# Two gated attentions and two feed-forward nets on one core: row maxima moved by DMA into the query tile, other lists for the first attention's engines, the second attention's first queries made in the FFN before it

## The reference

```python
q = x @ Wq.T + bq
k = context @ Wk.T + bk
v = context @ Wv.T + bv
...
scores = jnp.einsum('bhtd,bhcd->bhtc', q, k) / jnp.sqrt(jnp.asarray(d, x.dtype))
attn = jax.nn.softmax(scores, axis=-1)
out = jnp.einsum('bhtc,bhcd->bhtd', attn, v)
out = out.transpose(0, 2, 1, 3).reshape(B, T, D)
return out @ Wo.T + bo
```

## Time and profile before

| | us |
|---|---|
| median of 3 runs | 1145.16 |
| lowest and highest | 1142.67, 1146.78 |
| profiled execution | 1144.3 |
| its span in the trace | 1142.5 |
| granted PE clock, mean | 0.926 |

### The profile page before, as it was taken

How to read it: one execution, slowest core, us unless ns; L and a number is a source line. 1 busy time by engine, 2 the same in 40 slices (tenths; PEclk the granted TensorE clock), 3 DMA queues, 4 the chain that set the end, 5 groups by cost and what they waited for, 6 DMA issues and landing times. The chain is left out here.

```text
span 1142.5 us, 20567 instructions
## 1 busy us (share of the span) xinstructions
PE 987.9 (86%) x6833; PEld 864.7 (76%) x6833; DVE 792.5 (69%) x1588; ACT 626.8 (55%) x1088; POOL 235.1 (21%) x423
## 2 busy tenths in 40 slices
PE   6589999998659997826699995999999989999998
PEld 5367777776458876625588984899999977888888
DVE  5357888775339988979959833677777768656672
ACT  4156666665357779969748543556566544222230
POOL 4213333320139200000003303121111104111210
PEclk9699999999769999967689996999999998999999
DMA  6745554445042237779712376655656510000001
GB/s 200 220 107 140 134 133 116 128 121 163 1 159 111 111 123 223 252 254 325 258 45 100 126 240 137 165 119 118 127 127 132 123 38 1 20 19 33 23 19 38
DMA packets 102807, 143.60 MB, mean 126 GB/s; under 512 B 42950, under 2 KB 76742, under 8 KB 100438
## 3 DMA queue, kind: packets, MB, share of 16 engines
q1 hardware_dynamic: 102438, 141.67, 43.2%
q0 software_dynamic: 304, 1.10, 0.3%
HBM read 76.30 MB, written 47.13 MB: 108 GB/s over the span
## 5 line engine op out<-in xcount | busy, mean ns | idle before, releaser
L41 PE MATMUL bank<-f_xt_hi,f_w_hi 128*128 128x512 f32 x320 | 129.1, 404 | 14.3 <-DMA f_xt_lo<-x_spill 11.1
L43 PE MATMUL bank<-f_xt_hi,f_w_lo 128*128 128x512 f32 x320 | 126.5, 395 | 0.0
L42 PE MATMUL bank<-f_xt_lo,f_w_hi 128*128 128x512 f32 x320 | 126.3, 395 | 0.0
L2534 ACT ACTIVATE f_h<-bank,f_b 128x512 f32<-128x512 f32 x64 | 43.3, 690 | 121.8 <-PE bank L43 74.1
L595 ACT ACTIVATE a_prob<-bank 77x512 f32<-77x512 f32 x128 | 72.5, 591 | 31.5 <-PE bank L759 31.0
L661 DVE TENSOR_REDUCE a_maxima<-bank 128x4 f32<-128x308 f32 x128 | 60.4, 472 | 40.8 <-PE bank L734 40.5
L41 PEld LDWEIGHTS bank<-f_xt_hi,f_w_hi 128*128 128x128 f32 x320 | 61.2, 191 | 30.3 <-DMA f_xt_lo<-x_spill 13.5
L41 PE MATMUL bank<-f_w_hi,f_h_hi 128*128 128x256 f32 x256 | 72.6, 284 | 8.1 <-DVE xres L2499 8.1
L756 PE MATMUL bank<-a_stack,a_kb 96*77 96x256 f32 x256 | 70.8, 299 | 4.7 <-ACT a_mt L588 4.7
L43 PE MATMUL bank<-f_w_hi,f_h_lo 128*128 128x256 f32 x256 | 72.3, 282 | 0.0
L42 PE MATMUL bank<-f_w_lo,f_h_hi 128*128 128x256 f32 x256 | 72.3, 282 | 0.0
(11 more groups left out here) (299 smaller groups left out, 3081.1 us busy)
## 6 DMA issues: line engine op xcount, KB each, us to landing
u_spill<-f_ubuf SPq DMA_DIRECT2D x48, 256.0 KB, 2.6
f_uback<-u_spill SPq DMA_DIRECT2D x24, 512.0 KB, 5.8
a_stack<-a_queries SPq DMA_DIRECT2D x16, 512.0 KB, 4.8
a_q_max<-a_q_hi SPq DMA_DIRECT2D x32, 256.0 KB, 5.0
a_kb<-a_key_spill SPq DMA_DIRECT2D x96, 77.0 KB, 2.5
f_mats<-in_low_steps SPq DMA_DIRECT2D x12, 512.0 KB, 6.8
xres<-in_x SPq DMA_DIRECT2D x16, 256.0 KB, 4.4
a_queries<-a_q_hi SPq DMA_DIRECT2D x16, 256.0 KB, 2.6
```

Source lines behind the costliest of these rows:

```text
L41: nc.tensor.matmul(out, w_hi, m_hi, start=start, stop=False)
L42: nc.tensor.matmul(out, w_hi, m_lo, start=False, stop=False)
L43: return nc.tensor.matmul(out, w_lo, m_hi, start=False, stop=stop)
L2534: act.activation(h[:, n % 2, :], hbank[n % 4][:, :], ACT.Gelu, bias=b1[:, n:n + 1]).then_inc(h_ready, 1)
```

## The change

1. `stack` and `kb` have their free rows 96 to 111 filled: `kb` with the picks (once, in the set-up, by ACT for both halves of the double buffer), `stack` with the maxima. ACT copies the maxima as before and then issues a DMA that writes them to all 8 pairs of heads, 128 KB. A head's scores are one matmul over 112 rows; `s0` waits for that DMA instead of the copy. `pick` and its memset, and the memset of `mt`, go.
2. `PE_SLOT`, `ACT_SLOT`, `DVE_SLOT` and `POOL_SLOT` have another order, and the slots before batch 0 have lists of their own with the order that they had.
3. `fw` sends one of twelve pieces of the quantised weights, 196 KB, in each of the slots 1 to 12.
4. The layer norm, transpose and query products of the second attention's batch 0 are made in the quantised net's last block; the steps in `late_attention` return at once for batch 0. The half of `kz` that batch 0 uses is cleared and filled there as well, and the keys in `kz` and in `kb` have separate semaphores. The memset of `q_max` stands at the start of the block.

```diff
-                act.activation(pick[0:HEADS, :, :], pick_raw[:], ACT.Copy).then_inc(picked, 1)
+                for par in range(2):
+                    act.activation(kb[ROWS:FULL, par, :, :, :],
+                                   pick_raw[ROWS:FULL, :, :].rearrange("p (q a) s -> p a q s", a=2),
+                                   ACT.Copy).then_inc(picked, 1)
...
-        PE_SLOT = "s0 s1 t3 xt p1 s2 mx0 at0 s3 t0 mx1 s4 p3 mx2 s5 mx3 t1 pr0 s6 mx4 pr1 p5 mx5 s7 mx6 q0 p7 mx7 q1 mt t2".split()
-        ACT_SLOT = "s0 s1 p1 s2 at0 s3 p3 xt s4 s5 s6 st2 p5 s7 xn p7 mt q1".split()
-        DVE_SLOT = "w0 norm w1 mx0 w2 as mx1 mx2 xs mx3 ln mx4 w3 pu mx5 st1 mx6 am mx7 w4 w5 qs".split()
-        POOL_SLOT = "ln st1 xn".split()
+        PE_SLOT = "mx0 xt t3 mx1 s0 s1 mx2 s2 s3 p1 s4 mx3 s5 p3 mx4 s6 s7 at0 mx5 q0 mx6 q1 p5 mx7 pr0 t0 mt pr1 t1 t2 p7".split()
+        ACT_SLOT = "xt s0 s1 s2 s3 p1 s4 s5 st2 s6 at0 p3 q1 mt p5 s7 xn p7".split()
+        DVE_SLOT = "mx0 w0 w1 mx1 norm mx2 ln mx3 xs w2 mx4 w3 mx5 w4 as mx6 w5 mx7 qs am pu st1".split()
+        POOL_SLOT = "ln xn st1".split()
...
+                for what in early if isinstance(b, int) and b < 0 else order:
                     if what[0] == "w":
                         if not isinstance(b, int) or 0 <= b < FW_PIECES:
                             step(what, b, par)
                     elif what == "fw":
-                        if isinstance(b, int) and b == FW_PIECES:
-                            step(what, b, par)
+                        if not isinstance(b, int) or 1 <= b <= FW_PIECES:
+                            step(what, b - 1, 1 - par)
...
-                    sp.wait_ge(fw_done, FW_PIECES)
-                    for n in range(3):
-                        sp.dma_start(ffn["quantised"][:, n, :], fw[:, n * FW:(n + 1) * FW]).then_inc(fw_sent, 16)
-
-            slots(sp, SP_SLOT, step)
-            sp.wait_ge(fw_sent, 48)
+                    sp.wait_ge(fw_done, b + 1)
+                    sp.sem_inc(sp_passed, 1)
+                    n = fw_code.shape[1]
+                    sp.dma_start(ffn["quantised"].rearrange("p n f -> p (n f)")[:, bass.ds(b * n, n)],
+                                 fw[:, bass.ds(b * n, n)]).then_inc(fw_sent, 16)
+
+            slots(sp, SP_SLOT, step, SP_SLOT)
+            sp.wait_ge(fw_sent, 16 * FW_PIECES)
...
                     act.activation(mt[0:HEADS, par, :], MX[0:HEADS, 0:T], ACT.Copy).then_inc(mt_copied, 1)
+                    act.wait_ge(mt_copied, b + 1)
+                    act.dma_start(stack[ROWS:FULL, par, :, :].bitcast(F32),
+                                  mt[0:HEADS, par, :].bitcast(F32).unsqueeze(1).to_broadcast([HEADS, PAIRS, T]),
+                                  ).then_inc(mt_moved[par], 16)
...
                     if n == 0:
-                        pe.wait_ge(mt_copied, b + 1)
+                        wait_turn(pe, mt_moved, 16, b, par)
                         if isinstance(b, int) and b == 0:
-                            pe.wait_ge(picked, 1)
-                            pe.wait_ge(cleared, 3)
+                            pe.wait_ge(picked, 2)
                     if not (isinstance(b, int) and b == 0 and n < 2):
 
                         pe.wait_ge(probs, b * PAIRS + n - 1)
                     for half in range(2):
                         pair, a = pair_of(2 * n + half)
                         out = (S0, S1)[n % 2][0:S, half * T:(half + 1) * T]
-                        pe.matmul(out, kb[0:ROWS, par, a, pair, 0:S], stack[0:ROWS, par, pair, :],
-                                  start=True, stop=False)
-
-                        last = pe.matmul(out, pick[:, 2 * pair + a, 0:S], mt[:, par, :], start=False, stop=True)
+                        last = pe.matmul(out, kb[0:FULL, par, a, pair, 0:S], stack[0:FULL, par, pair, :],
+                                         start=True, stop=True)
                     last.then_inc(scores, 1)
...
-                    for a in range(HPC):
-                        sp.dma_start(kz[own[a], par, :, a, :].bitcast(F32),
-                                     late["k_dram"][own[a], 0, :, bass.ds(b * S, S)]).then_inc(keys_in[par], 16)
+                    for a in range(HPC if not (isinstance(b, int) and b == 0) else 0):
+                        sp.dma_start(kz[par][own[a], :, a, :].bitcast(F32),
+                                     late["k_dram"][own[a], 0, :, bass.ds(b * S, S)]).then_inc(kz_in[par], 16)
+                    if isinstance(b, int) and b < 2:
+                        sp.wait_ge(picked, b + 1)
...
+                    if i == 1:
+                        pool.wait_ge(ocoded, late["values_free"] - 4)
+                        pool.memset(late["kz0"][:].bitcast(F32), 0.0).then_inc(first.kz_cleared, 1)
+                pool.wait_ge(first.cleared, 3)
+                pool.wait_ge(first.ln_stats, 1)
+                pool.tensor_tensor(first.nmean[:], first.zero[:], first.mv[:, :, 0], ALU.subtract)
+                pool.tensor_tensor(first.var[:], first.mv[:, :, 1], first.eps[:], ALU.add).then_inc(first.ln_eps, 1)
+                pool.wait_ge(first.ln_eps, 1)
+                pool.tensor_tensor(first.rstd[:], first.var[:], first.minus_half[:], ALU.pow).then_inc(first.ln_rstd, 1)
+                pool.wait_ge(first.ln_rstd, 1)
+                pool.tensor_tensor(first.nmr[:], first.nmean[:], first.rstd[:], ALU.mult).then_inc(first.ln_nmr, 1)
...
+                    if i == 2:
+                        sp.wait_ge(first.kz_cleared, 1)
+                        for n in range(2):
+                            sp.wait_ge(k_saved[n], 16 * NK)
+                        for a in range(2):
+                            half = slice(a * P // 2, (a + 1) * P // 2)
+                            sp.dma_start(late["kz0"][half, :, a, :].bitcast(F32),
+                                         late["k_dram"][half, 0, :, 0:S]).then_inc(first.kz_in[0], 16)
...
+                    if b == 12:
+                        dve.wait_ge(e_added, 1)
+                        for t in range(TT):
+                            last = dve.bn_stats(first.bn[:, t, :], xres[:, t, :])
+                        last.then_inc(first.ln_bn, 1)
+                        dve.wait_ge(first.ln_bn, 1)
+                        for t in range(TT):
+                            last = dve.bn_aggr(first.mv[:, t, :], first.bn[:, t, :])
+                        last.then_inc(first.ln_stats, 1)
+                    if b == 14:
+                        dve.wait_ge(first.xt_rounded, 1)
+                        dve.tensor_tensor(xt_lo, T1[:, :].rearrange("p (c t) -> p c t", c=DC), xt_hi.bitcast(F32),
+                                          ALU.subtract).then_inc(first.xt_split, 1)
...
+                    if b == 14:
+                        act.wait_ge(first.ln_nmr, 1)
+                        for t in range(TT):
+                            last = act.activation(xn[:, t, :], xres[:, t, :], ACT.Identity,
+                                                  bias=first.nmr[:, t:t + 1], scale=first.rstd[:, t:t + 1])
+                        last.then_inc(first.ln_xn, 1)
+                    if b == 16:
+                        act.wait_ge(first.xt_ready, 1)
+                        act.activation(xt_hi, T1[:, :].rearrange("p (c t) -> p c t", c=DC), ACT.Copy).then_inc(first.xt_rounded, 1)
...
+                    if b == 14:
+                        pe.wait_ge(first.ln_xn, 1)
+                        pe.wait_ge(v_done, 7)
+                        for c in range(DC):
+                            for t in range(TT):
+                                last = pe.transpose(T1[:, c * T + t * P:c * T + (t + 1) * P],
+                                                    xn[:, t, c * P:(c + 1) * P], ident[:])
+                        last.then_inc(first.xt_ready, 1)
+                pe.wait_ge(first.xt_split, 1)
+                pe.wait_ge(l_split["wq"], 1)
+                pe.wait_ge(v_done, 8)
+                pe.wait_ge(e_added, B - 1)
+                for n in range(2):
+                    for c in range(2):
+                        cols = slice((2 * n + c) * P, (2 * n + c + 1) * P)
+                        for kc in range(DC):
+                            last = three_passes(nc, (T0, X0)[n][:, c * T:(c + 1) * T], late["wq_hi"][:, kc, cols],
+                                                late["wq_lo"][:, kc, cols], xt_hi[:, kc, :],
+                                                xt_lo[:, kc, :], kc == 0, kc == DC - 1)
+                    last.then_inc(first.q_ready, 1)
```

122 lines of the change are left out of this document (76 added, 46 removed).

## The result

The changed kernel is slower. It takes 1164.8 us in the median of four runs (1158.81 to 1172.57), beside 1145.97 for the kernel before in the same comparison; the ratio is 1.0156, with a 95% interval of 1.0121 to 1.0191. The forecast was 1125, the range ended at 1138, and the time lies 27 us above it. The profiled execution took 1162.29 us with a span of 1160.5, 18.0 more than the span of 1142.5 before, at a mean granted clock of 0.899 instead of 0.926.

A forecast was written before the change was run, and what follows sets the result against it. PE was taken to set the pace, busy 14.34 of a 15.0 us slot, DVE next. Terms -22.5 + 1.1 + 0.5 - 1.0 - 0.5 (keys' wait) + 2.1 = -20.3 gave 1125 us, range 1114 to 1138.

The forecast's parts named there:

- Matmuls removed: First attention's slots: dropping 16 matmuls a batch shortens twelve slots to 13.6 us and three to 13.1, -22.5 us.
- The maxima's DMA: Before s0 in each slot: the landing, taken as 2.6 us, fits in 3.3 us, so it costs 0.
- transfer rival: First attention's slots: maxima or keys land 0.7 us too late in each, +10.5 us, 1136 in all; chance 0.17.
- The clock falls: Rival, first attention's slots: 3 us of each at half clock, +18 us, 1143, no change; chance 0.05.
- The slower case: Rival, s0 of each batch: maxima land like the slowest key transfer, 2.8 us late, +42 us, 1167; chance 0.07.
- Set-up: Before the first attention: ACT copies the picks twice, 1.23 us each, delaying PE's start, +1.1 us.
- First slot: Slot 0: first s0 waits for a landing instead of a copy, with less between, +0.5 us (0 to +2.5).
- Tail: Emptying pipeline after the last mt: 16 matmuls fewer, but a DMA landing hardly covered, -1 us (-3 to +1).
- First queries in the FFN: FFN end and late attention's start: next block +8.5 us later, first s0 then -6.4, sum +2.1 us.

The follow-up runs named there:

- last set: Changed kernel with s0 and s1 by two matmuls, s2 to s7 from the DMA, fillers, other early lists: 1191.1 us; also s3, s5 made twice: 1215.8 us.

## Why the prediction was wrong

- **Matmuls removed: right in its place.** "I lay it at 13.6 us": slots at full clock with pieces of the weights in them last 13.6 to 14.3, and the two at or near full clock behind them 13.6 and 13.3, for 13.1. Fifteen such slots make about 206, for 202.5. PE has 12.5 to 12.75 us of work in them, for 12.4.
- **The maxima's DMA: "I take 0" failed, and the row it came from was misread.** The landing is 4.0 us in the median, 3.0 to 5.8, where I took 2.6 from the earlier trace rows as that of "77 KB transfers of keys". That row puts together two kinds. The list of transfers of the kernel before keeps them apart (count, size, median us to landing):

```profile
a_kb<-a_key_spill SPq DMA_DIRECT2D x96, 77.0 KB, 2.5
...
a_kb<-a_keys SPq DMA_DIRECT2D x96, 39.0 KB, 4.3
```

The 77 KB are the second attention's. In the first attention, where the new DMA runs, half as much took 4.3 us, more than the 3.3 us that I had to hide it in; by this row the maxima would land 1.0 us late in each slot, above the transfer rival's 0.7. In fact s0 came 4.7 us after mt and not 4.2, since t2's wait of 0.7 us lies between, and so it waits where the landing took 3.9 us or more, in eight of the last thirteen slots, 7.2 us in all.
- **The clock: here the prediction broke.** The rival "The clock falls" had the right mechanism, with 3 us at half clock a slot, +18 us and a chance of 0.05. There were 92 us at half clock, some 6 a slot, and 39 us lost. I ruled it out by "a window with PE busy 12.9 of 15 stays at 1.00", as if the sum of idle time decided. It does not: the slots that fell in the changed kernel have 1.2 to 2.8 us of idle time, and that window of the kernel before has 2.1 and a slot without L759 2.2 in small pieces, both at full clock. In the changed kernel it stands in two pieces of 0.7 and 0.3 to 1.6 us within five microseconds. I had also priced each rival alone, while the transfer rival's wait goes with the clock's falls.
- **The slower case** that I did name (landing at 4.9 us or more) was not needed: 4.0 was enough, by way of the clock.
- **Set-up +1.1:** +1.6, the two copies take 2.39 in place of 1.23. **First slot +0.5:** s0 comes 4.8 us after mt where it was 1.0, and half clock follows from 66 to 97 us, which no term had; the first two slots took 36.7 us, for 29.4 in the kernel before. **Tail -1:** +2.0.
- **First queries in the FFN: right in its steps.** ACT's wait for nmr is there (3.80), f_o_hi(15) comes 4.3 us later against wq's rounding (4.5 forecast), 24 products run mostly at 0.21, the first s0 comes 13.1 us after its block starts (13.05 forecast, though its own terms add up to 12.95). The net is +0.1 for +2.1, since the block starts 6.4 later, not 8.5. Without this part the time is the same (1165.6).
- **The Trainium skill's rule** (DMA: Bandwidth & Descriptors, "Issuing engines are not separate DMA queues"), that a transfer issued on ACT shares the engines with SP's, is not contradicted by the trace: the maxima's 4.0 us is about the landing of the keys in the same stage, issued on SP (3.9 in the changed kernel, 4.3 before). It pointed the right way where the row as I read it did not. No run moved the issue to SP, so how much of the 4.0 is due to sharing was not tried.

The cause as far as the runs show it: half clock is what the forecast's slots lost, and PE's waits around the turn of a slot bring it in the changed kernel. Filled, the falls stop (1150.7); with the DMA's wait taken out, most of them do (1153.5); put into the kernel before, a longer wait makes them appear (1177.2, though mostly by its own length); the DMA, the lists and the FFN part are not needed for it. The work in a slot seems to have a part in it: one wait of 0.6 to 1.4 us at 13.9 us of work was all but harmless, and one of 1.5 us at 12.5 was not; this compares single executions. The run with each score matmul twice varies the work with the waits kept, and had fewer falls. What stays open is which pattern is enough; the list with s7 and p5 ahead of mt, with shorter waits and more falls, and the last set, with none and seven falls of eleven, fit no account given here. Executions of one kernel near the edge differ by 13 to 17 us (1145 to 1158 without the DMA's wait, 1145 to 1162 without L759), and no version kept both the clock and the gain.

## What to carry to other kernels

TensorE's work in a full pipeline can also hold its clock: before taking matmuls away, look where the idle time will stand, in one piece or in many, and price a slot at both clocks. Cut the span at a marker that comes once per iteration and list the intervals; a mean of 16.4 us hid slots of 13.8 and 18.2. A wait of half a microsecond for a transfer is not half a microsecond if the clock follows, so a landing should be taken with its spread, from transfers of the same stage and not from a row that mixes two stages, and what hides it should be longer than its tail.

## What was not expected of the hardware

- 256 matmuls fewer, with nothing added, made the kernel 1% slower (1158.3 for 1145.7), and 20 unread matmuls a batch more (with 16 in slot 0 and the other early lists) made the changed one 14 us faster.
- Half clock lasts longer than the wait ahead of it: 1.5 us of waiting up to 137 and ten microseconds at half clock behind it, with PE busy throughout from 140 on.
- Matmuls over 16 and 96 rows in turn start 0.27 us apart, those over 96 and 128 rows 0.12.
- ACT writes from partitions 0 to 15 of a bank into partitions 96 to 111 of SBUF: two copies of 1024 columns in 1.92 us, against 4.0 for the DMA's landing.
